# Moving the shared expert of a mixture-of-experts layer from the third phase to the first, and running the first norm of the second layer ahead, in a two-layer decoder on one core

## The chip, the core and the metric

The kernel runs on 1 of the 8 cores of one Trainium2 chip. The metric is the device time of one execution in microseconds. TensorE (PE) does the matmuls and loads its weights beside them (PEld); VectorE (DVE), ScalarE (ACT) and GpSimd (POOL) work on what it leaves; SyncE (SP) issues nearly all DMAs. Each engine runs its own instruction stream in order, and the streams meet at semaphores.

## What is computed

Sixteen sequences of 256 tokens of 128 features pass through two layers; ctx is 64 tokens of 96 features for each sequence.

```python
x = ln(x + L0_attn(x))            # 16 heads of 8, causal
x = ln(x + L0_xattn(x, ctx))      # 8 heads of 16
x = ln(x + L0_ffn(x))             # router: 6 of 64 experts, at most 64 tokens each, and the shared expert
x = ln(x + L1_attn(x))            # 16 heads of 64, causal
x = ln(x + L1_xattn(x, ctx))      # 16 heads of 64
x = ln(x + L1_ffn(x))             # attention over four nested slices, 8 heads of 16
# in L0_ffn the shared expert, the part that the change moves:
z = silu(xf @ ws1.T) * (xf @ ws3.T) @ ws2.T      # 128 -> 176 -> 128 features
return (y + z).reshape(shape)                    # y: the sum of the six experts of each token
```

## The kernel before, in words

Everything is fp32 but the scores from which only row maxima are taken. The program has three parts, since an expert can only run when all tokens have been routed.

**Phase one** (`phase1_streams`) takes the sequences in pairs, A (s = 0) and B (s = 1), through L0 and L0X and the router R, 8 iterations. It stores the tokens with their router scores in `xg` in DRAM (192 columns a token, one store a sequence, step RN on SP). **The experts** gather token rows from `xg`, run, and scatter into `zd` (six rows a token). **Phase three** (`phase3_streams`) takes the pairs through the rest. For each sequence it loads the token (`x3_in`) and its six rows (`routed`), and then runs the steps "F": XT transposes the tokens on PE; F1 is the two products with ws1 and ws3, a tanh on ACT and two fused DVE operations; F2 is the product with ws2 and the DVE addition; Z on DVE sums the six rows and adds the token; then come the norm (statistics on DVE, the power of -0.5 on POOL, step L on DVE), and layer 1: XT, Q, K, V, S (scores for the maxima), N (their transpose), T (transposed scores and exp), P (values), D and B (row sums), W (output product).

**The order** of all this is written out by hand. Each phase has four streams of steps, two main ones (A and B) and two of the router or of XT-F1-Z (C and D). A string of turns (`TURNS1`, `TURNS3`) says which stream gives the next step. `AHEAD` says how many steps of each stream belong to the next pair: with (5, 19, 3, 3) the loop body runs the last 79 and 65 steps of the main streams for its own pair and the first 5 and 19 for the next one. Every engine walks the same list. Ahead of the loop the list is walked once for the "ahead" steps alone, and behind it once for the others alone.

PSUM has six units, which rings of the names Q, O, D and M share out (`fills` gives the ring of each step). A unit has a semaphore for full and one for free, and counts must go on where a step is left out. So PE does `absent_step` for every step that the walk leaves out (L917 to L922):

```python
for i in range(len(fills(step))):
    pe.wait_ge(*v.may_fill(step, i))
    pe.sem_inc(v.full(step, i), 1)
    pe.sem_inc(v.free(step, i), 1)
```

That is three instructions of PE's sequencer for each fill. Line numbers below are those of the kernel before: the transpose XT is L506, F1 L904, F2 L913, the product Q L522, K L535, the largest score L1143, exp L1016, Z L1279 and L1283, the norm L1056 to L1075 and L1313, W of L1F L858.

Of the kernel before, what the change touches and what calls it, by code (L numbers as in the profile page):

```python
# [5 lines left out]
FP32 = mybir.dt.float32  # L6
# [11 lines left out]
FI = 88  # L18
# [88 lines left out]
def phase3_streams():  # L107
    shared = lambda s: [("XT", "F", s, 0), ("F1", "F", s, 0), ("Z", "F", s, 0)]
    main = lambda s: ([("F2", "F", s, 0), ("L", "F", s, 0), ("XT", L1, s, 0)] + project_steps(L1, s) + head_steps(L1, s)
# [3 lines left out]
    return [main(s) for s in AB] + [shared(s) for s in AB]  # L113


TURNS1 = ("A B A B A C A4 B A2 B A2 C B2 A D A B C A D B A2 D B C B4 D A B C A B D B D A2 B A B A2 D B A B A "
          "B2 A B D A B A2 B4 A B2 A D A B2 A B2 A2 B2 A")
TURNS3 = ("B A B2 A2 B2 A5 B A B A3 B2 A3 B A B3 A4 B3 A B8 A B3 A3 B A B A B A B A B3 A2 B2 A B A2 B A4 B A3 "
          "B2 A2 B A3 B A B A2 B A B A B A B A4 B2 A2 B A2 B A B2 A B2 A D A B A B A D B C A2 B A B A B A B A "
          "D B3 A2 C A3 B2 A C A B5 A B2 A B4 A B3 A2 B2")  # L120
AHEAD1, AHEAD3 = (36, 31, 0, 0), (5, 19, 3, 3)
# [25 lines left out]
def fills(step):  # L147
# [17 lines left out]
    if kind in ("D", "L", "C", "CK", "RN", "RL", "Z") or kind == "W" and step[3]:  # L165
        return []
# [22 lines left out]
def decoder_program(nc, inp, out):  # L189
    ctx = ExitStack()  # L190
    with ctx:
# [12 lines left out]
        zd = nc.dram_tensor("zd", [TOK * TOPK, D], FP32, kind="Internal").ap()  # L204

# [26 lines left out]
        wx_o2 = sb("wx_o2", [128, 2, 128])  # L232
        wx_o = wx_o2[:, 0, :]
# [4 lines left out]
        ws2 = wx_o2[0:FI, :, :]  # L238
# [8 lines left out]
        w1x_o = sb("w1x_o", [128, 8, 128])  # L247
        b1x_o = sb("b1x_o", [128, 128])
# [57 lines left out]
        rstd = pair("rstd", [128, 4])  # L306
        eps = sb("eps", [128, 4])
# [3 lines left out]
        hid_e = [t[0:FI, 1, 0:512].rearrange("p (c t) -> p c t", c=2) for t in v_big]  # L311

# [27 lines left out]
        class Sync:  # L340


            def __init__(self, tag):
# [16 lines left out]
                if tag == "p1":  # L360
# [4 lines left out]
                    self.key_moved = n("key_moved")  # L365
                    self.sorted = sem(f"{tag}_sorted")
                else:
# [3 lines left out]
                    self.z_link = n("z_link")  # L371
                    self.once_added = n("once_added")
                    self.scaled = n("scaled")
                    self.h_act = n("h_act")
                    self.z_sum = n("z_sum")
# [6 lines left out]
               ("p3", "F"): 0, ("p3", L1): 1, ("p3", L1X): 2, ("p3", L1F): 3}  # L382
        LN_PER = {"p1": 2, "p3": 4}
# [85 lines left out]
        def previous_x(a):  # L469

            return {L0X: L0, "R": L0X, L1: "F", L1X: L1, L1F: L1X}[a]

        def x_source(tag, a, s):

            if a == "F":
                return x3_in[s][:, :, :]
# [13 lines left out]
        def tensor_step(pe, v, step):  # L490
            kind, a, s = step[0], step[1], step[2]
            y, mm = v.y, nc.tensor.matmul
            if kind == "XT":
                if a == "F":
                    pe.wait_ge(y.x_in[s], v.at(16, 16))
                    if not v.first():

                        pe.wait_ge(y.x_ready[s], v.ln(L1X) - LN_PER["p3"])
# [399 lines left out]
            elif kind == "F1":  # L898
                if not v.follows(step, ("XT", "F", s, 0)):
                    pe.wait_ge(*v.drained(("XT", "F", s, 0)))  # L900
                for i in range(2):
                    pe.wait_ge(*v.may_fill(step, i))
                    for c in range(2):
                        last = mm(v.bank(step, i)[0:FI, c * 256:(c + 1) * 256], ws13[:, 2 * i + c, :], xt[s][:, :],  # L904
                                  start=True, stop=True)
                    last.then_inc(v.full(step, i), 1)
            elif kind == "F2":
                if not v.follows(step, ("F1", "F", s, 0), 0, 1):
                    pe.wait_ge(*v.drained(("F1", "F", s, 0), 1))
# [14 lines left out]
        def scalar_step(act, v, step):  # L924
# [27 lines left out]
            elif kind == "K":  # L952
                i, bank = step[3], v.bank(step)
                act.wait_ge(*v.filled(step))
                if a is L1:
                    for j in range(2):
# [122 lines left out]
        def vector_step(dve, v, step):  # L1079
# [111 lines left out]
            elif kind == "L":  # L1191
                if a is L0X:
# [675 lines left out]
```

## Time and profile before

| | |
|---|---|
| time before, median of 3 runs | 2123.05 us (2116.55 to 2128.08) |
| the profiled execution | 2126.89 us, its span 2124.9 us |
| busy, share of the span | PE 82%, PEld 52%, DVE 53%, ACT 42%, POOL 11% |
| mean granted TensorE clock | 0.912 of full speed |
| phase one | about 22 to 558 us |
| the experts | about 558 to 670 us |
| phase three | about 670 us to the end; outputs of a pair 174.0 to 177.5 us apart |

Times are microseconds from the start of the span. A busy PE need not be PE at its peak, since ends of matmuls are modelled. "Idle before" names what ended an engine's idle time; "issue" is time in which it waited for nothing that the profile shows, and PEq is PE's own sequencer.

### The profile page before, as it was taken

Reading aid. Unit: us, or ns where it says so; the run is one execution under the profiler, and the core shown is the slowest. Engines: PE = TensorE matmul, PEld = TensorE weight load, DVE = VectorE, ACT = ScalarE, POOL = GpSimd, SP = SyncE. Lnnn points to the kernel's source line nnn. Section 1 sums busy time; section 2 is a strip of 40 time slices with the busy share of each in tenths; the row PEclk is TensorE's granted clock in tenths of the full one; section 3 lists DMA queues with packets and bytes.
Section 4 is the critical chain, followed back from the end, with each engine's and each line's share of the span. In section 5 each row is a group of like instructions: output and inputs, shape, how many; then the busy total and the mean of one; then the engine's idle time right before and its main releaser. Section 6 shows DMA issues by size and latency. Waiting matters only on the chain.

```text
span 2124.9 us, 49983 instructions
## 1 busy us (share of the span) xinstructions
PE 1741.2 (82%) x20036; PEld 1104.7 (52%) x20052; DVE 1126.7 (53%) x2330; ACT 894.5 (42%) x1625; POOL 228.2 (11%) x392
## 2 busy tenths in 40 slices
PE   3787777777263699899799889989979978988995
PEld 2444444444153366456556556655745655664663
DVE  5567766777532434643662563464356257256434
ACT  2444444454110245444444444544444445445453
POOL 0100011010074000100100100010010010001000
PEclk9879988999575799999999899989989999998998
DMA  8200000000373100100000010010000001000000
GB/s 295 105 16 19 18 18 7 19 14 7 96 92 93 35 2 3 41 2 3 21 22 2 2 41 2 2 40 2 4 21 22 2 2 41 2 2 6 1 2 6
DMA packets 43295, 60.23 MB, mean 28 GB/s; under 512 B 6183, under 2 KB 33297, under 8 KB 42659
## 3 DMA queue, kind: packets, MB, share of 16 engines
q1 hardware_dynamic: 40003, 53.95, 7.9%
q0 software_dynamic: 2560, 3.46, 1.8%
q8 instruction: 141, 2.31, 0.5%
q10 hardware_dynamic: 576, 0.39, 0.1%
q14 instruction: 15, 0.12, 0.0%
HBM read 39.63 MB, written 19.92 MB: 28 GB/s over the span
## 4 chain that ended last, share of the span: by engine, by line
PE 68%; ACT 10%; DVE 9%; issue 8%; DMA 2%; POOL 2%; PEldq 1%; ACTq 0%; DVEq 0%; SPq 0%; POOLq 0%
PE psum L522 7%; PE psum L749 6%; PE psum L864 6%; PE psum L661 5%; ACT prob L1016 5%; PE psum L714 4%; DVE peak L1143 3%; PE psum L547 3%; PE psum L535 3%; PE psum L762 3%; PE psum L817 3%; PE psum L904 2%; PE psum L579 2%; PE psum L656 2%; PE psum L614 2%
## 5 line engine op out<-in xcount | busy, mean ns | idle before, releaser
L1016 ACT ACTIVATE prob<-psum 128x1024 f32<-128x1024 f32 (+2 forms) x384 | 339.9, 915 | 385.8 <-PE psum L668 176.8
L1143 DVE TENSOR_REDUCE peak<-psum 128x4 bf16<-128x1024 f32 (+2 forms) x304 | 366.0, 1223 | 165.7 <-PE psum L590 97.3
L1310 POOL TENSOR_TENSOR rstd<-moments,eps 128x2 f32<-128x2 f32 x96 | 18.7, 195 | 1554.1 <-DVE moments L1061 1554.1
L661 PE MATMUL psum<-qt,kt 64*128 64x256 f32 x1024 | 131.8, 377 | 0.0
L1126 DVE TENSOR_REDUCE peak<-psum 128x8 bf16<-128x512 f32 x64 | 41.3, 688 | 158.5 <-PE psum L597 158.5
L749 PE MATMUL psum<-prob,v_big 128*64 128x256 f32 x1024 | 124.6, 385 | 0.0
L614 PE MATMUL psum<-kb,qb 32*128 32x512 bf16 x320 | 64.3, 416 | 62.1 <-DVE peak L1143 35.8
L1150 DVE RECIPROCAL rsum<-psum 128x128 f32<-128x128 f32 x32 | 30.7, 958 | 152.9 <-PE psum L762 111.7
L714 PE MATMUL psum<-qt,kt 32*128 32x256 f32 (+1 forms) x1536 | 103.4, 392 | 0.0
L817 PE MATMUL psum<-prob,va 128*32 128x256 f32 (+1 forms) x1536 | 97.0, 374 | 5.1 <-ACT prob L1016 4.9
L1172 DVE TENSOR_TENSOR qt<-qt,psum 128x1024 f32<-128x1024 f32 x64 | 78.0, 1219 | 34.5 <-PE psum L844 34.5
L661 PEld LDWEIGHTS psum<-qt,kt 64*128 64x128 f32 x1024 | 87.4, 188 | 8.0
L714 PEld LDWEIGHTS psum<-qt,kt 32*128 32x128 f32 x1536 | 87.5, 218 | 7.0
L973 ACT CAST qb<-qt 128x1024 bf16<-128x1024 f32 (+1 forms) x112 | 86.6, 773 | 1.3
L749 PEld LDWEIGHTS psum<-prob,v_big 128*64 128x64 f32 x1024 | 67.8, 136 | 36.6 <-issue 4.2
L958 ACT ACTIVATE kt<-psum,b_qk 128x256 f32<-128x256 f32 x128 | 53.6, 470 | 78.6 <-PE psum L535 78.2
L1187 DVE TENSOR_TENSOR summed<-psum,x_res 128x256 f32<-128x256 f32 x80 | 33.9, 423 | 80.3 <-PE psum L864 49.2
L535 PE MATMUL psum<-xt,w_qkv 128*128 128x256 f32 x256 | 74.6, 421 | 0.5
L1313 POOL TENSOR_TENSOR rstd<-rstd,power 128x2 f32<-128x2 f32 (+1 forms) x96 | 72.6, 757 | 7.5
L710 PE MATMUL psum<-shift_n,sel_h 32*128 32x384 bf16 (+1 forms) x384 | 39.2, 396 | 40.8 <-ACT prob L1016 20.2
L547 PE MATMUL psum<-w_qkv,xt 128*128 128x512 f32 x128 | 72.3, 648 | 0.0
L864 PE MATMUL psum<-w1x_o,qt 128*128 128x128 f32 x512 | 64.8, 280 | 8.2 <-DVE qt L1172 8.2
(246 smaller groups left out, 3311.1 us busy)
## 6 DMA issues: line engine op xcount, KB each, us to landing
zd<-kx SPq DMA_DIRECT2D x24, 512.0 KB, 6.0
union<-zd SPq DMA_DIRECT2D x16, 768.0 KB, 4.6
xg<-union SPq DMA_DIRECT2D x16, 192.0 KB, 2.0
v_big<-in_w1T SPq DMA_DIRECT2D x4, 704.0 KB, 8.8
prob<-in_w3T SPq DMA_DIRECT2D x4, 704.0 KB, 11.5
kt<-in_w2T SPq DMA_DIRECT2D x4, 704.0 KB
union<-in_x SPq DMA_DIRECT2D x16, 128.0 KB, 2.2
union<-in_xT SPq DMA_DIRECT2D x16, 128.0 KB, 2.2
```

Of the source, the lines that this page charges most:

```text
L522: last = mm(bank[:, j * 256:(j + 1) * 256], w[:, c * 128:(c + 1) * 128], x, start=True, stop=True)
L535: last = mm(bank[:, j * 256:(j + 1) * 256], w1_qkv[:, c * 128:(c + 1) * 128], xt[s][:, :], start=True, stop=True)
L547: last = mm(bank[:, :], xt[s][:, t * 128:(t + 1) * 128], w1_qkv[:, 2048 + 512 * half:2560 + 512 * half], start=True, stop=True)
L614: last = mm(banks[:, jj, :].rearrange("p (i k) -> p i k", i=heads.stop - heads.start), qb[s][r, 0, q0:q0 + 128], kb[s][r, heads, keys], st ...
L661: mm(banks[:, u, j * 256:(j + 1) * 256], kt[s][r, c, ktile * 128:(ktile + 1) * 128], qt[s][r, c, :], start=False, stop=False, skip_group_c ...
L714: last = mm(bank[:, 256 * k:256 * k + 256 - q0], km[a][s][r, g, 128 * k:128 * k + 128], qt[s][r, 0, q0:256], start=False, stop=a is L1F, s ...
L749: last = mm(bank[64 * u:64 * u + 64, j * 256:(j + 1) * 256], v_big[s][:, k, h * 64:(h + 1) * 64], prob[s][:, slot + 2 * k + u, j * 256:(j ...
L817: last = mm(bank[32 * j:32 * j + 32, c + q0:c + 256], lhs, p, start=(g == 0 and k == 0), stop=(k == 1), skip_group_check=True)
L864: last = mm(bank[:, t * 128:(t + 1) * 128], qt[s][:, u, t * 128:(t + 1) * 128], w[:, u, :], start=(u == 0 and t == 0), stop=(u == 7), skip ...
L973: copy(flat(qb[s][:, c, :]), flat(qt[s][:, c, :])).then_inc(y.q16[s], 1)
L1016: nc.scalar.activation(prob[s][:, slot + 2 * i:slot + 2 * i + 2, 0:n], v.pair(step, i)[:, :, 0:n], ACT.Exp, scale=a.scale).then_inc(v.free ...
L1143: nc.vector.tensor_reduce(dst, src, axis=AX.X, op=ALU.max).then_inc(v.free(step), 1)
```

## The change

The shared expert (F1, F2) becomes part of the router's stream in phase one, where it uses the transposed tokens that the router has made. Its output, with the token added, is stored in a new DRAM array `xz` (F2 on SP), and phase three loads `xz` in place of the token columns of `xg`. In phase three a new stream "front" holds Z (the sum of six rows), Y (the addition and the statistics, with semaphores and tiles of their own), L (the norm, in place in `x_ffn`) and the transpose of layer 1's input. All four run ahead for the next pair; the transpose of the tokens for F1 is gone. Turns and AHEAD are new. `w1x_o` holds L0X's output weight in phase one, so L1_Wo is loaded behind the routers, and ws13 and ws2 at the start.

```diff
-    router = lambda s: ([("XT", "R", s, 0)] + [(k, "R", s, 0) for k in ("R1", "RN", "R2", "R3")]
+    router = lambda s: ([("XT", "R", s, 0)] + [(k, "R", s, 0) for k in ("R1", "F1", "RN", "F2", "R2", "R3")]
-    shared = lambda s: [("XT", "F", s, 0), ("F1", "F", s, 0), ("Z", "F", s, 0)]
-    main = lambda s: ([("F2", "F", s, 0), ("L", "F", s, 0), ("XT", L1, s, 0)] + project_steps(L1, s) + head_steps(L1, s)
+    front = lambda s: [("Z", "F", s, 0), ("Y", "F", s, 0), ("L", "F", s, 0), ("XT", L1, s, 0)]
+    main = lambda s: (project_steps(L1, s) + head_steps(L1, s)
-AHEAD1, AHEAD3 = (36, 31, 0, 0), (5, 19, 3, 3)
+AHEAD1, AHEAD3 = (29, 36, 0, 0), (43, 46, 4, 4)
...
+                dve.wait_ge(y.xz_kept[s], v.at(16, 1))
+                tt(xz_out[s], v.bank(step)[:, 0:256].rearrange("p (t d) -> p t d", t=2), xs[s][:, :, 0:D],
+                   ALU.add).then_inc(v.free(step), 1)
+            elif kind == "Z":
                 if not v.first():
-                    dve.wait_ge(y.x_ready[s], v.ln(L1F) - LN_PER["p3"])
...
+                    dve.wait_ge(y.x_ready[s], v.ln(L1X) - LN_PER["p3"])
+                dve.wait_ge(y.routed_in[s], v.at(16, 16))
+                nc.vector.tensor_reduce(x_ffn[s], routed[s].rearrange("p t k d -> p t d k"), axis=AX.X,
+                                        op=ALU.add).then_inc(y.f_link[s], 1)
+            elif kind == "Y":
+                dve.wait_ge(y.f_link[s], v.at(3, 1))
+                dve.wait_ge(y.x_in[s], v.at(16, 16))
+                tt(x_ffn[s], x_ffn[s], x3_in[s][:, :, :], ALU.add).then_inc(y.f_link[s], 1)
...
+            elif kind == "F2":
+                sp.wait_ge(*v.drained(step))
+                sp.dma_start(xz[bass.ds(seq * T, T), :].rearrange("(t p) w -> p t w", p=128), xz_out[s]).then_inc(
+                    y.xz_kept[s], 16)
...
             for q in AB:
                 sp.wait_ge(p1.r_keyed[q], ITERS)
+                sp.wait_ge(p1.xz_kept[q], ITERS * 16 + 1)
```

Three places of PE's order, before and after. Names end in the sequence's number (1 is B, 0 is A), and ident, psum and the weights are common. The first place is the start of phase three, behind the last expert; before:

```order
L506 MATMUL psum<-ident,x3_in1 128x128 x2
L904 MATMUL psum<-xt1,ws13 88x256 x4
L506 MATMUL psum<-ident,x3_in0 128x128 x2
L913 MATMUL psum<-wx_o2,v_big1 128x128 x4
L904 MATMUL psum<-xt0,ws13 88x256 x4
L506 MATMUL psum<-ident,x_tok1 128x128 x2
L522 MATMUL psum<-xt1,w1_qkv 128x256 x4
```

and after, where the new lines L510, L526 and L539 are the old L506, L522 and L535:

```order
L510 MATMUL psum<-ident,kt1 128x128 x2
L526 MATMUL psum<-xt1,w1_qkv 128x256 x4
L539 MATMUL psum<-xt1,w1_qkv 128x256 x4
L510 MATMUL psum<-ident,kt0 128x128 x2
L526 MATMUL psum<-xt1,w1_qkv 128x256 x2
```

The five rows of F ahead of layer 1's first transpose are gone, and that transpose reads the normed tokens in `kt1` at once. The second place is the loop of phase three, in the last module L1F of both sequences; before:

```order
L858 MATMUL psum<-wf_o,kt1 64x128 x4
L913 MATMUL psum<-wx_o2,v_big1 128x128 x4
L690 REGISTER_ALU
L710 MATMUL psum<-shift_n0,sel_h 128x512 x4
L714 MATMUL psum<-qt0,kt0 128x256 x8
L817 MATMUL psum<-prob0,va0 32x256 x8
L904 MATMUL psum<-xt0,ws13 88x256 x2
L902 REGISTER_ALU
L904 MATMUL psum<-xt0,ws13 88x256 x2
L736 REGISTER_ALU
L817 MATMUL psum<-prob0,va0 32x256 x8
```

and after, where L862, L714, L718 and L821 are the old L858, L710, L714 and L817:

```order
L862 MATMUL psum<-wf_o,kt1 64x128 x4
L526 MATMUL psum<-xt1,w1_qkv 128x256 x4
L653 REGISTER_ALU
L714 MATMUL psum<-shift_n0,sel_h 128x512 x4
L718 MATMUL psum<-qt0,kt0 128x256 x8
L821 MATMUL psum<-prob0,va0 32x256 x8
L533 REGISTER_ALU
L539 MATMUL psum<-xt1,w1_qkv 128x256 x4
L507 REGISTER_ALU
L510 MATMUL psum<-ident,kt0 128x128 x2
L740 REGISTER_ALU
L821 MATMUL psum<-prob0,va0 32x256 x8
```

Where F1 and F2 stood between the products of A's L1F, the next B's Q and K of layer 1 stand now. The third place is the loop of phase one; after, with L908 the F1 and L917 the F2 of phase one:

```order
L908 MATMUL psum<-x_out0,ws13 88x256 x2
L906 REGISTER_ALU
L908 MATMUL psum<-x_out0,ws13 88x256 x2
L653 REGISTER_ALU
L714 MATMUL psum<-shift_n1,sel_h 128x384 x4
L718 MATMUL psum<-qt1,kt1 128x256 x4
L718 MATMUL psum<-qt1,kt1 128x128 x4
L728 MATMUL psum<-tri_t,ident_inf 32x2x128 x16
L917 MATMUL psum<-ws2,v_big1 128x128 x4
```

Here F1 of A is followed, one T step later, by F2 of B. Before, no row of ws13 stood in this loop.

## Rows read from the trace of the kernel before

**Rows 1.** Windows: us, busy us (instructions) of PE, PEld, DVE, ACT, POOL, clock, DMA.

```profile
95.40:485.00 389.60, 305.90 (x4426) 180.21 (x4436) 274.72 (x682) 179.00 (x397) 38.68 (x72) 0.89 0.05 16
...
886.00:1940.50 1054.50, 957.00 (x10297) 609.04 (x10296) 531.21 (x936) 482.38 (x805) 85.58 (x168) 0.95 0.05 14
...
1940.50:2124.90 184.40, 157.22 (x1726) 99.80 (x1724) 86.52 (x161) 80.99 (x134) 15.16 (x30) 0.94 0.02 4
```

**Rows 2.** Waits of PE, 886 to 1940.5 us: total, times, longest.

```profile
PE psum L522 <- ACT xt_nested L933: 14.3, 12, 1.4
```

**Rows 3.** Timeline of PE around L1F: start, us, instruction, idle before it.

```profile
1212.37 2.08 PE L522 MATMUL psum<-xt_nested,w_qkv 128*128 128x256 f32 x4 [0.93 <-ACT xt_nested L933]
...
1219.70 3.71 PE L904 MATMUL psum<-xt,ws 128*88 128x256 f32 x8
...
1236.62 2.02 PE L904 MATMUL psum<-xt,ws 128*88 128x256 f32 x8
...
1247.51 1.13 PE L913 MATMUL psum<-wx_o,v_big 88*128 88x128 f32 x8 [0.15 <-ACT kt L958]
```

**Rows 4.** Groups by line: count, busy us, mean ns, idle before.

```profile
L904 PE MATMUL psum<-xt,ws 128*88 128x256 f32 x128 | 46.3, 525 | 1.8 <-PEq L922 1.8
...
L913 PE MATMUL psum<-wx_o,v_big 88*128 88x128 f32 x128 | 19.2, 296 | 5.1 <-PEq L922 3.8 <-ACT kt L958 1.2
```

**Rows 5.** Timeline at the start of phase three.

```profile
669.29 0.48 DVE L1783 MEMSET va<- 128x512 f32 x1
...
678.06 0.90 SPq L1344 DMA_DIRECT2D union<-zd  x2
...
702.56 0.66 PE L506 MATMUL psum<-ident,x_in 128*128 128x128 f32 x2 [37.41 <-PEq L922]
...
705.04 3.44 PE L904 MATMUL psum<-xt,ws 128*88 128x256 f32 x8 [1.81 <-PEq L922]
...
708.51 0.41 PE L506 MATMUL psum<-ident,x_in 128*128 128x128 f32 x2
...
709.19 2.73 DVE L1279 TENSOR_REDUCE kt<-union 128x256 f32<-128x1536 f32 x1
711.95 0.43 DVE L1283 TENSOR_TENSOR kt<-kt,x_in 128x256 f32<-128x256 f32 x1
...
712.76 2.05 PE L913 MATMUL psum<-wx_o,v_big 88*128 88x128 f32 x8 [3.84 <-PEq L922]
...
714.60 3.62 PE L904 MATMUL psum<-xt,ws 128*88 128x256 f32 x8
...
719.58 0.44 PE L506 MATMUL psum<-ident,x_tok 128*128 128x128 f32 x2 [1.36 <-DVE x_tok L1075]
```

**Rows 6.** Timeline of DVE's part of F.

```profile
714.85 0.42 DVE L1289 TENSOR_TENSOR summed<-psum,kt 128x256 f32<-128x256 f32 x1 [2.47 <-PE psum L913]
...
717.18 0.68 DVE L1272 SCALAR_TENSOR_TENSOR v_big<-v_big,psum 88x512 f32<-88x512 f32 x1 [0.99 <-ACT v_big L1049]
```

**Rows 7.** Timeline of the end.

```profile
2116.23 0.66 PE L858 MATMUL psum<-wf_o,kt 128*64 128x128 f32 x8 [0.46 <-ACT kt L1037]
...
2117.39 0.49 DVE L1056 BATCH_NORM_STATS2 stats<-summed 128x6 f32<-128x128 f32 x2
...
2119.44 0.60 DVE L1075 TENSOR_SCALAR x_out<-summed,moments,rstd 128x128 f32<-128x128 f32 x2 [1.16 <-POOL rstd L1313]
```

**Rows 8.** DMA issues: count, KB each, median us from issue to landing.

```profile
union<-zd SPq DMA_DIRECT2D x16, 768.0 KB, 4.6
xg<-union SPq DMA_DIRECT2D x16, 192.0 KB, 2.0
```

**Rows 9.** Timeline of the first waits for weights and for DVE.

```profile
15.52 1.50 POOL L1328 TENSOR_TENSOR x_res<-union,b_o 128x256 f32<-128x256 f32 x2 [14.59 <-DMA x_in<-in_token_key]
...
21.95 2.08 PE L522 MATMUL psum<-union,w_qkv 128*128 128x256 f32 x4 [21.95 <-DVE sel_h L1768]
```

**Rows 10.** The chain that ended last, between routers and experts: start, us.

```profile
569.53 8.92 DMA summed<-kx
```

More of the change, by code:

```diff
@@ L164, in fills @@
         return ["Q"]
-    if kind in ("D", "L", "C", "CK", "RN", "RL", "Z") or kind == "W" and step[3]:
+    if kind in ("D", "L", "C", "CK", "RN", "RL", "Z", "Y") or kind == "W" and step[3]:
         return []
@@ L469, in previous_x @@
         def previous_x(a):
-            return {L0X: L0, "R": L0X, L1: "F", L1X: L1, L1F: L1X}[a]
+            return {L0X: L0, "R": L0X, L1X: L1, L1F: L1X}[a]
         def x_source(tag, a, s):
-            if a == "F":
-                return x3_in[s][:, :, :]
+            if a is L1:
+                return x_ffn[s]
             if a == "R":
@@ L493, in tensor_step @@
             if kind == "XT":
[L494 to L498, printed above, removed]
+                if a is L1:
+                    pe.wait_ge(y.f_x_ready[s], v.once())
                 elif a is L1F:
@@ L903, in tensor_step @@
                     for c in range(2):
-                        last = mm(v.bank(step, i)[0:FI, c * 256:(c + 1) * 256], ws13[:, 2 * i + c, :], xt[s][:, :],
+                        last = mm(v.bank(step, i)[0:FI, c * 256:(c + 1) * 256], ws13[:, 2 * i + c, :], r_xt[s],
                                   start=True, stop=True)
@@ L1191, in vector_step @@
             elif kind == "L":
-                if a is L0X:
+                if a == "F":
+                    dve.wait_ge(y.f_rstd_ready[s], v.at(2, 2))
+                    for t in range(2):
+                        last = nc.vector.tensor_scalar(x_ffn[s][:, t, :], x_ffn[s][:, t, :], moments_f[s][:, t, 0:1],
+                                                       rstd_f[s][:, t:t + 1], ALU.subtract, ALU.mult)
+                    last.then_inc(y.f_x_ready[s], 1)
+                elif a is L0X:
                     dve.wait_ge(y.out_done[s], v.at(16, 1))
+                    dve.wait_ge(y.xz_kept[s], v.at(16, 1))
                     layer_norm_apply(dve, v, s, a, summed[s], xs[s][:, :, 0:D])
@@ L1291, in vector_step @@
-                dve.wait_ge(*v.drained(step))
-                layer_norm_sums(dve, v, s, "F", summed[s])
+                    dve.wait_ge(y.x_ready[s], v.ln(L1X) - LN_PER["p3"])
[6 more added lines that the diff above has]
+                tt(x_ffn[s], x_ffn[s], x3_in[s][:, :, :], ALU.add).then_inc(y.f_link[s], 1)
+                dve.wait_ge(y.f_link[s], v.at(3, 2))
+                for t in range(2):
+                    last = nc.vector.bn_stats(stats_f[s][:, t, :], x_ffn[s][:, t, :])
+                last.then_inc(y.f_link[s], 1)
+                dve.wait_ge(y.f_link[s], v.at(3, 3))
+                carry_wait(dve)
+                for t in range(2):
+                    last = nc.vector.bn_aggr(moments_f[s][:, t, :], stats_f[s][:, t, :])
+                last.then_inc(y.f_moments_ready[s], 1)
@@ L1299, in pool_step @@
             y = v.y
-            if kind == "F2" or kind == "W" and (step[3] or not a.big):
-                which = "F" if kind == "F2" else a
+            if kind == "Y":
+                pool.wait_ge(y.f_moments_ready[s], v.once())
+                nc.gpsimd.tensor_tensor(rstd_f[s][:, :], moments_f[s][:, :, 1], eps[:, 0:2], ALU.add).then_inc(
+                    y.f_rstd_ready[s], 1)
+                pool.wait_ge(y.f_rstd_ready[s], v.at(2, 1))
+                nc.gpsimd.tensor_tensor(rstd_f[s][:, :], rstd_f[s][:, :], power[:, 0:2], ALU.pow).then_inc(
+                    y.f_rstd_ready[s], 1)
+            if kind == "W" and (step[3] or not a.big):
+                which = a
                 pool.wait_ge(y.moments_ready[s], v.ln(which))
```

84 lines of the change are left out of this document (41 added, 43 removed).

## The prediction

> **What bounds the kernel now.** I read the span in windows first, one for the loop of each phase. Six iterations of phase three take 1054.5 us, 175.75 each, and PE is busy for 957.0 of them (91%); DVE is busy for 531 and ACT for 482 [rows 1]. So phase three is bound by PE, and work taken off PE there is worth nearly its own time. Six iterations of phase one take 389.6 us, 64.9 each: PE 305.9 (79%), DVE 274.7 (71%), ACT 179.0 [rows 1]. No engine is full there; PE and DVE hand the lead to each other, and per iteration PE has (389.6 - 305.9) / 6 = 14.0 us of idle time and DVE 19.1. What work added there costs depends on where it falls. The second view is the waits of PE in phase three's loop. The largest is for the nested input of L1F, 14.3 us in 12 waits [rows 2], and the timeline shows the same place in one iteration: PE comes to it late and at the lower clock level. The four matmuls of Q there take 2.08 us, and F1, which comes 7 us later as PE's filler, takes 3.71 us, while the other F1 of the same pair takes 2.02 [rows 3]: half the clock, 1.2 for 2.4 GHz. The third view is the timeline of the two ends. PE is free for phase three when DVE's last memset ends at 669.77, but its first matmul stands at 702.56, and the idle time is its own sequencer's [rows 5].
>
> **Head of phase three.** That idle time is absent_step. In the order before, 106 fills of left-out steps come ahead of the first ahead step: (702.56 - 669.77) / 106 = 0.31 us a fill. After, counted from the new turns in the same way, 54 fills stand there, 16.7 us, so that PE arrives at 686.5. The data are then what is late. The rows of the experts are asked for at 678.06 to 678.96 [rows 5] and land in 4.6 us [rows 8], B's at about 683.1. Z takes 2.7 us, the addition 0.4 [rows 5], links 0.35 in all, and statistics to the end of the norm 2119.44 + 0.60 - 2117.39 = 2.65 us, as at the end of the run [rows 7]. That gives 689.3. The first transpose of layer 1 starts at about 689.7 for 719.58 [rows 5]: **-29.9**. If the landing is 3 us later, 3 us less.
>
> **Work taken off PE in phase three.** Per sequence one transpose, F1 and F2. Over the whole phase F1 is busy for 46.3 us and F2 for 19.2 [rows 4]; sixteen transposes at 0.41 to 0.66 [rows 5] are about 8. Together 73.5 us. Of them 0.66 + 3.44 + 0.41 + 2.05 + 3.62 = 10.2 us stand ahead of 719.58 [rows 5] and are in the first term, so at most 63.3 remain. F1 has its mean of 2.9 us by the low clock of one of two; at full clock a sequence costs 2.02 + 1.13 + 0.44 = 3.59 [rows 3, 5], sixteen of them 57.4, less 6.0 for the same pieces, 51.4. Which it is depends on whether the low stretch goes on to lie on other matmuls. I take the middle: **-57**, 7.1 us an iteration. The transpose of layer 1's input, Z, the additions and the norm stay, on their engines; DVE loses 0.68 + 0.68 + 0.42 a sequence [rows 6], which no one waits for. The norm had no slack before: PE waited 1.36 us for it at 719.58 [rows 5]. It now runs at least ten PE rows ahead of its Q.
>
> **The gaps of L1F.** F was filler there. In the new order the first half of L1F (from Q of B to T of B) has none in its place, and the second half has the next B's Q and K, which are more work than F was. I set the change of the gaps at 0, with -5 to +4 us an iteration as the bounds: the whole wait for the nested input is 14.3 / 6 = 2.4 us an iteration [rows 2], the idle time of an iteration 16.2 [rows 1], and I do not expect a third of it to go or a quarter more to come.
>
> **Tail of phase three.** The new AHEAD is paid at the other end. The walk behind the loop leaves out 89 main and 8 front steps, and 69 fills of them come behind the last W of A; before, it was 18. At 0.31 us a fill 69 are 21.3 us on PE's sequencer, and the program ends when PE does. Before, the end came at 2124.9, 8.0 us behind the last row of L858 (2116.23 + 0.66) [rows 7], through the norm and the last store; 18 fills are 5.6 and hid behind those. So **+13.3**, up to +16 at the 0.35 us a fill that the wait for F2 shows (3.84 us, 11 fills) [rows 5].
>
> **Phase one.** Added per iteration: on PE 2 x (2.02 + 1.13) = 6.3 us at full clock, 2 x (3.62 + 2.05) = 11.3 at half [rows 3, 5]; on DVE 3.6 [rows 6]; two stores of 128 KB, which land in about 2.0 us as the 192 KB ones do [rows 8]. SP waits in its queue for F2's drain ahead of the store; queued behind it are the other sequence's xg store, then context loads that are needed an iteration later, so this wait costs nothing. L0X's norm waits for the previous store, a whole iteration old. No row shows F in this loop, so I bound it. From below: PE has 14.0 us idle per iteration [rows 1], most of it in pieces shorter than F1, and a denser PE could raise the 0.89 of its clock; -1 us an iteration. From above: all of it exposed at the low clock, and 2 us for the ring M, because F2 of B waits for the unit that F1 of A has just filled and DVE empties only behind RN: 13 us. The loop keeps an engine 79% busy, so I take half of the 6.3 exposed and 1.3 for the ring: 4.5 us, times eight, **+36**. At the end of phase one the pieces of F stand in the last chain of A, and L1_Wo adds 424 KB to the loads ahead of the half list, whose move took 8.92 us on the chain [rows 10] against 2.0 for a larger store [rows 8]: together **+5** (0 to 10). At the start ws13 and ws2 join the weights that PE waits for. The last of these now landed by 15.52, and DVE held PE until 21.95 [rows 9]: 6.4 us of cover for two issues and 264 KB. Nothing; if that cover were gone they would cost 2 to 3.
>
> **The sum.** -29.9 - 57 + 13.3 + 36 + 5 = -32.6, against the profiled execution's own 2126.9: 2094. That execution stands 3.8 above the median of the runs shown, so I forecast **2090 us**, 1.5% less.
>
> **The clock, weighed.** The loop's granted clock is 0.95, and in the place where F1 was filler it is at the lower level [rows 1, 3]. If the gaps there grow, more of the iteration runs at that level. Should the mean fall to 0.91, an iteration loses 175 x 0.04 = 7 us, 56 in all, and the sum would be 2146. By the Trainium skill ("TensorE: Matmul & The Clock Gate", Part 1, HAM oscillation) idle gaps of PE throttle it back to half rate, and the work behind each gap then runs slowly until activity has released it again; it speaks against taking filler out of a latency-bound stretch. By that rule the trace agrees, in that Q behind a gap takes twice its time. I hold to the sum since the second half of L1F gets new filler.
>
> **The rivals.**
> 1. F was filler, and its removal saves little. Then an iteration gives 3 us, not 7.1, and the time is 2090 + 33 = 2123, no change. For it: F1 at 1219.70 lies in a stretch where PE waits anyway. Against it: the other F1, at 2.02 us, and both F2 lie in full stretches. 0.13.
> 2. The new order closes gaps as well: the second half of L1F, with Q, K and S of the next B beside it, loses 4 us of idle an iteration; seven of them give 28 and 2062. For it: 16.2 us of idle, and a front that no longer stands in the chain. Against: the first half. 0.17.
> 3. Slower: phase one takes F at its full low-clock price with the waits of ring M, 13 us an iteration; +68 on the forecast, 2158. It decides against the change from 9.8 us an iteration on. For it: F2 of B directly behind F1 of A. Against: 14 us of idle and a clock that density raises. 0.07.
> 4. The clock, above: 2146. 0.05.
>
> **How the numbers follow.** The forecast has 0.58, with its own range of 2070 to 2110. 0.5% of the time, 10.6 us, is about what a measurement of this kernel can tell from no change. Faster by more than that: 0.58 + 0.17 and a little of rival 1: 0.76. Same: 0.13. Slower: 0.11. The range for 8 in 10 leaves out the lowest of rival 2 and rivals 3 and 4: 2052 to 2125.
>
> **What would show it.** First transpose of layer 1 at 688 to 694 (shifted by what phase one gained); some 55 fills of sequencer time ahead of it. PE's last matmul 20 to 25 us ahead of the span's end. Period of phase three 168 to 170 us, clock at 0.95. Period of phase one 68 to 71, with waits of F2 for DVE. The prediction is wrong if the period of phase three stays above 173 or falls under 164, or if phase one grows by less than 1 or more than 9 us an iteration.

## The result and the profile after

The changed kernel took 2134.35 us (median of 20 runs) beside 2120.2 us for the kernel before on the same chip. The ratio is 1.0063, with an interval of 1.0040 to 1.0086: **slower by 0.6%**, where 1.5% faster was forecast. The profiled execution has a span of 2128.3 us against 2124.9, and a clock of 0.895.

Windows of the changed kernel (us, busy us and instructions of each engine, clock, DMA share, GB/s): five periods of phase one from x load to x load, the rest of phase one, six iterations of phase three.

```profile
105.42:466.63 361.21, 290.00 (x3822) 171.70 (x3831) 243.06 (x596) 157.73 (x340) 32.26 (x60) 0.87 0.07 20
466.63:628.09 161.46, 129.19 (x1554) 77.63 (x1556) 106.92 (x283) 65.05 (x145) 13.10 (x25) 0.81 0.06 18
930.34:1936.80 1006.46, 920.10 (x10084) 587.42 (x10080) 511.99 (x900) 469.50 (x781) 89.07 (x169) 0.95 0.05 14
```

Phase three has fallen from 175.75 us an iteration [rows 1] to 1006.46 / 6 = 167.7, at the same clock. Phase one has grown to 361.21 / 5 = 72.2. The kernel before has 64.9 by the same marks, the window here:

```profile
95.42:420.06 324.64, 256.88 (x3662) 151.57 (x3670) 226.05 (x566) 148.88 (x330) 32.24 (x60) 0.87 0.05 16
```

At the start of phase three, the timeline of the changed kernel answers to [rows 5]. At its end, it answers to [rows 7]:

```profile
740.38 0.48 DVE L1812 MEMSET va<- 128x512 f32 x1
749.15 0.90 SPq L1371 DMA_DIRECT2D union<-zd  x2
755.28 2.74 DVE L1299 TENSOR_REDUCE kt<-union 128x256 f32<-128x1536 f32 x1 [14.41 <-DMA union<-zd]
760.58 0.60 DVE L1201 TENSOR_SCALAR kt<-kt,moments_f,rstd_f 128x128 f32<-128x128 f32 x2 [1.18 <-POOL rstd_f L1323]
761.24 0.69 PE L510 MATMUL psum<-ident,kt 128*128 128x128 f32 x2 [24.99 <-DVE kt L1201]
...
2106.11 0.74 PE L862 MATMUL psum<-wf_o,kt 128*64 128x128 f32 x8 [0.46 <-ACT kt L1043]
```

PE now waits for DVE's norm (L1201), no longer for its own sequencer, and starts layer 1 at 761.24, 20.4 us behind the last memset; before it was 49.8. At the end its last matmul stands at 2106.85 and the span ends at 2128.3, 21.4 us later.

With these marks the 3.4 us by which the spans differ are made up completely:

| stretch | before | after | difference |
|---|---|---|---|
| start to the expert loads | 558.78 | 628.09 | +69.3 |
| to the request of the experts' rows (678.06, 749.15) | 119.3 | 121.1 | +1.8 |
| to the first transpose of layer 1 (719.58, 761.24) | 41.5 | 12.1 | -29.4 |
| to PE's last matmul (2116.89, 2106.85) | 1397.3 | 1345.6 | -51.7 |
| to the end | 8.0 | 21.4 | +13.4 |

Four of five stretches lie within 5.3 us of the forecast. The error is in the first: +69.3, where +36 and a part of the +5 were given. Two things stand out in it. The first is the timeline of PE at the place where the loop of phase one begins anew (behind W of L0X for B, L875):

```profile
305.63 0.71 PE L875 MATMUL psum<-w1x_o,kt 128*128 128x128 f32 x4 [0.46 <-ACT kt L1043]
309.94 0.40 PE L644 MATMUL psum<-neg_ident,peak 128*32 128x128 bf16 x8 [3.60 <-issue]
311.00 0.44 PE L699 MATMUL psum<-shift_n,sel_h 32*64 32x256 bf16 x8 [0.66 <-ACT shift_n L1010]
311.19 1.09 PE L703 MATMUL psum<-qt,kt 32*64 32x256 f32 x5
312.64 1.15 PE L703 MATMUL psum<-qt,kt 32*64 32x256 f32 x11 [0.36 <-issue]
313.71 2.08 PE L526 MATMUL psum<-union,w_qkv 128*128 128x256 f32 x4
315.72 1.98 PE L808 MATMUL psum<-prob,vx 128*64 128x256 f32 x8
```

"<-issue" is idle time in which PE waited for nothing that the profile shows: 3.6 us, and 0.36 inside a step that is one row elsewhere. Q behind it takes 2.08 us, nearly twice what it takes at the higher clock level. At the first entry into the loop the same steps follow one another with none of this (L875 at 96.40, L644 at 97.04, Q at 98.67 in 1.13 us): W to Q takes 2.3 us there and 8.1 here. The second is the queue of code in the list of DMA queues (packets, MB, share of 16 engines). It is first the kernel before, then the changed one:

```profile
q8 instruction: 141, 2.31, 0.5%
```

```profile
q8 instruction: 195, 3.19, 0.6%
```

### The profile page after: what moved, and what is told of

Read it like the earlier page. It is cut to its first block, busy times and chain, and to the rows that moved or that the text cites. A ratio compares the mean times of both kernels' runs of the same rounds, so it can differ in the third digit from the quotient of the medians.

```text
span 2128.3 us, 49852 instructions
## 1 busy us (share of the span) xinstructions
PE 1762.4 (83%) x20004; PEld 1116.8 (52%) x20020; DVE 1128.5 (53%) x2330; ACT 891.2 (42%) x1609; POOL 234.7 (11%) x392
## 4 chain that ended last, share of the span: by engine, by line
PE 59%; issue 16%; DVE 14%; ACT 5%; POOL 3%; DMA 2%; SPq 1%; DVEq 0%; ACTq 0%; PEldq 0%; POOLq 0%; PEld 0%
PE psum L753 6%; PE psum L526 5%; DVE peak L1149 5%; PE psum L665 5%; PE psum L868 4%; PE psum L718 3%; PE psum L766 3%; PE psum L551 3%; PE psum L539 3%; PE psum L660 2%; ACT prob L1022 2%; PE psum L583 2%; PE psum L821 2%; PE psum L543 1%; PE psum L618 1%
## 5 line engine op out<-in xcount | busy, mean ns | idle before, releaser
L718 PE MATMUL psum<-qt,kt 32*128 32x256 f32 (+1 forms) x1536 | 107.0, 402 | 0.0
L618 PE MATMUL psum<-kb,qb 32*128 32x512 bf16 x320 | 72.5, 450 | 40.6 <-ACT prob L1022 16.2
L821 PE MATMUL psum<-prob,va 128*32 128x256 f32 (+1 forms) x1536 | 93.6, 363 | 1.8 <-ACT prob L1022 1.6
L718 PEld LDWEIGHTS psum<-qt,kt 32*128 32x128 f32 x1536 | 88.9, 222 | 7.8
L1193 DVE TENSOR_TENSOR summed<-psum,x_res 128x256 f32<-128x256 f32 x80 | 33.8, 423 | 99.3 <-PE psum L868 71.6
L954 ACT COPY qt<-psum 128x512 f32<-128x512 f32 x80 | 46.2, 585 | 81.0 <-PE psum L526 80.0
L526 PE MATMUL psum<-xt,w1x_q 128*128 128x256 f32 x256 | 66.6, 406 | 14.2 <-issue 10.5
L1029 ACT COPY qt<-psum 128x512 f32<-128x512 f32 x64 | 37.5, 585 | 91.3 <-PE psum L753 91.1
L526 PE MATMUL psum<-xt,w_qkv 128*128 128x256 f32 x256 | 70.2, 408 | 2.8 <-PEq L926 2.1
L539 PE MATMUL psum<-xt,w_qkv 128*128 128x256 f32 x256 | 69.8, 401 | 1.1 <-PEq L926 0.6
```

The source lines that it names most:

```text
L526: last = mm(bank[:, j * 256:(j + 1) * 256], w[:, c * 128:(c + 1) * 128], x, start=True, stop=True)
L539: last = mm(bank[:, j * 256:(j + 1) * 256], w1_qkv[:, c * 128:(c + 1) * 128], xt[s][:, :], start=True, stop=True)
L618: last = mm(banks[:, jj, :].rearrange("p (i k) -> p i k", i=heads.stop - heads.start), qb[s][r, 0, q0:q0 + 128], kb[s][r, heads, keys], st ...
L718: last = mm(bank[:, 256 * k:256 * k + 256 - q0], km[a][s][r, g, 128 * k:128 * k + 128], qt[s][r, 0, q0:256], start=False, stop=a is L1F, s ...
L821: last = mm(bank[32 * j:32 * j + 32, c + q0:c + 256], lhs, p, start=(g == 0 and k == 0), stop=(k == 1), skip_group_check=True)
```

## The experiments

Chips differ in the stage of the experts: from its loads to the request of its rows it took 119 to 124 us on some and 144 to 152 on others, for kernels of either order. So stages are compared by their own marks, and whole times by the ratio to the kernel before on the same chip. "Period" is always the mean of five, from x load to x load, as in the windows above; the expectations name some periods up to 1 us shorter (71.6 and 63.9 for 72.2 and 64.9). Theory 1 at first was that PE's branch back costs several us when nothing is queued behind which it hides; its rival (theory 2) was that F's own work is all of the growth.

**1. The loop cut elsewhere.**

```diff
-TURNS1 = ("A2 B A B A D B3 ... A2 B A2 B2 D B")
-AHEAD1 = (29, 36, 0, 0)
+TURNS1 = ("B A B A D B3 ... A2 B A2 B2 D B A2")
+AHEAD1 = (31, 36, 0, 0)
```

> The changed kernel with the loop of phase one cut at another place: the steps N and T of L0X for sequence A, first in the loop's body, stand at its end instead (AHEAD1 31 for 29), so that PE branches back with 16 + 48 instructions of work queued and not with one W. The order of the work is the same. Theory 1 (the back branch of PE's loop costs 4 to 6 us where nothing is queued behind which it hides): the loop's period in phase one falls from 71.6 to 66-68 us, phase one by 28-42 us, the kernel from 2134 to about 2095-2105. Theory 2 (F's own work is all of the growth): period 71.6 +/- 0.5, the kernel within 5 us of the changed one.

The period was 338.86 / 5 = 67.8 us and the expert loads began at 597.89, 30.2 us earlier. Ratio 0.9896 (0.9854 to 0.9938). The same work in the same order was 1.7% shorter, which theory 2 does not allow.

**2. The cut of the kernel before, moved to behind W.**

```diff
-TURNS1 = ("A B A B ... B A2 B2 A")
-AHEAD1 = (36, 31, 0, 0)
+TURNS1 = ("B2 A A B A B ... B A2")
+AHEAD1 = (35, 29, 0, 0)
```

> The kernel before with the cut of phase one's loop moved the other way: N and T of L0X for B and the last L of A stand at the start of the body instead of at its end (AHEAD1 35, 29), so that the loop ends behind L0X's W, with nothing queued. Same work in the same order. Theory 1: the period in phase one grows from 63.9 to 68-70 us, the kernel by 28-42 us (ratio 1.013 to 1.02). Theory 2: 63.9 +/- 0.5 us, ratio 1.000 +/- 0.003.

Period 318.72 / 5 = 63.7 us, the expert loads at 558.34. Ratio 1.0036 (1.0006 to 1.0065), of which phase one shows nothing. With nothing queued at the branch PE ran on without a stall, so theory 1 falls in this form: the empty queue is not what costs.

**3. The order of before with F put in.**

```diff
+def with_f(plan):
+    out = []
+    for step, ahead in plan:
+        kind, a, s = step[0], step[1], step[2]
+        if kind == "R2":
+            out.append((("F2", "R", s, 0), 0))
+        out.append((step, ahead))
+        if a is L0 and (kind, s) in (("T", 0), ("P", 0)) and step[3] == 1:
+            out.append((("F1", "R", 0 if kind == "T" else 1, 0), 0))
+    return out
```

> The changed kernel with phase one in the order of the kernel before (its turns and its cut of the loop), F1 and F2 put in where they stand in no gap by intent: F1 for A behind T of L0's second round, for B behind the second P, F2 ahead of R2. Theory 1: with the cut behind queued work the period is 66-68 us and the kernel 2090-2105. Theory 2: F costs 7.7 us an iteration wherever it stands: period 71-72, the kernel 2125-2140. Theory 3 (the new order of phase one itself is slower, not F and not the cut): period 65-67 here, and the cut alone (the kernel with the loop cut elsewhere) gives nothing.

Period 363.00 / 5 = 72.6 us, expert loads at 631.70, ratio 1.0093 (1.0062 to 1.0124); 141 packets of code. F put into this order costs 72.6 - 64.9 = 7.7 us an iteration, nearly the 8.0 us by which phase three's iteration fell. It is what theory 2 said, but theory 2 had failed in experiment 1.

**4. The changed kernel without F.**

```diff
-        plan = {"p1": interleaved(phase1_streams(), TURNS1, AHEAD1),
+        plan = {"p1": [x for x in interleaved(phase1_streams(), TURNS1, AHEAD1)
+                       if x[0][0] not in ("F1", "F2")],
```

> The changed kernel without F1 and F2 in phase one on any engine, and without their store: the shared expert is left out of the result, phase three loads the tokens where it loaded their sum with the shared expert. Order and cut of the loop are the changed kernel's. Theory 1 (cut 4-6, F 2-4 us an iteration): the period falls to 68-70 us. Theory 2 (F is all of it): to 63.9-64.5. Theory 3 (the order): stays over 70.

Period 355.94 / 5 = 71.2 us, expert loads at 617.89, 136 packets, ratio 1.0011 (0.9979 to 1.0043). Only theory 3 gave such a period, and it had failed in experiments 1 and 3, where the cut alone gave 30 us and the old order nothing. Some 160 matmuls in five periods are gone, and the period is longer than that of experiment 1 with F.

**What the four have in common.** Of the kernels so far only the changed one has 195 packets; the others have 136 to 141, and none of theirs lie between 175 and 530 us. The queue of code of the changed kernel in that stretch:

```profile
q8 instruction: 44, 0.72, 0.8%
```

That is 9 packets of 16 KB in each iteration. PE's loop has 1,633 instructions of 64 bytes, 102 KB or 6.4 pieces of 16 KB; it is the only loop in the phase that is longer than a piece. The Trainium skill ("Runtime: NRT & Kernel Launch", Instruction fetch mechanics) says that PE holds 128 KB of code, refilled in blocks of 16 KB; a note there has only two blocks held and a fetch at every branch out of them. The traces here speak against the note: PE's loops of 98 and 102 KB jump back without a packet in every kernel so far but the changed one. By the figure of 128 KB a loop that touches seven blocks leaves one to fetch into, and one that touches eight leaves none. That was theory 4, and position alone tests it.

**5. Nothing but PE's code moved.**

```diff
+            for _ in range(80):
+                pe.sem_inc(pad, 1)
             pe.wait_ge(consts_ready, 1)
```

> The changed kernel with 80 increments of an unused semaphore ahead of PE's first wait, which ends at about 57 us and hides them. Nothing else differs; PE's code behind them lies 5,120 bytes further on. Theory 4 (code): the changed kernel's loop of phase one is fetched anew in every iteration (195 instruction packets of 16 KB in all, some 10 an iteration, against 141 and none between 170 and 580 us in the kernel before and in every kernel run so far), because of where its 1,633 instructions of 64 bytes begin in the 16 KB pieces of code; moved on, they stay. Then 141 packets or so, no stall of 3.6 us behind W of L0X, a period near 68.3 us as where the loop was cut elsewhere, the expert loads at 598-602 us instead of 628.1, the kernel 25-32 us shorter than the changed one (ratio about 0.99). Theory 1 (an empty queue at the back branch): no change, period 71.6, expert loads at 628, ratio 1.004 to 1.009.

Expert loads at 594.35, 33.7 us earlier; ratio 0.9875 (0.9831 to 0.9919). The page has

```profile
q8 instruction: 135, 2.21, 0.4%
```

and the window of the five periods, and PE where the loop begins anew, are

```profile
105.46:441.60 336.14, 280.41 (x3820) 170.47 (x3828) 242.53 (x595) 157.94 (x340) 32.33 (x60) 0.90 0.06 19
```

```profile
296.69 0.71 PE L875 MATMUL psum<-w1x_o,kt 128*128 128x128 f32 x4 [0.46 <-ACT kt L1043]
297.33 0.30 PE L644 MATMUL psum<-neg_ident,peak 128*32 128x128 bf16 x8
298.29 0.32 PE L699 MATMUL psum<-shift_n,sel_h 32*64 32x256 bf16 x8 [0.66 <-ACT shift_n L1010]
298.39 0.64 PE L703 MATMUL psum<-qt,kt 32*64 32x256 f32 x16
298.96 1.13 PE L526 MATMUL psum<-union,w_qkv 128*128 128x256 f32 x4
```

The stall is gone and Q behind it is at full clock; W to Q is 2.3 us, as in straight code. The period is 67.2 us for 72.2. The first x load of the loop is at 105.46 for 105.42, so the increments themselves cost nothing.

**6. The same edit, moved by a whole piece of 16 KB.** The number is 256 instead of 80.

> The changed kernel with 256 increments ahead of PE's first wait: 16,384 bytes, one whole piece of code, where 80 of them (5,120 bytes) ended the fetching in phase one's loop. Theory 4 (what counts is where the loop lies within its 16 KB pieces): the place within a piece is that of the changed kernel again, so the loop is fetched anew in every iteration: 190 to 200 packets, a period of 71 to 72 us, a stall of 3 to 5 us at the loop's start, expert loads at 625-630 us, ratio 1.003 to 1.01. Theory 5 (any shift of the start ends it, by other timing): about 140 packets, expert loads at 594-600, ratio 0.985 to 0.99.

196 packets, period 362.15 / 5 = 72.4 us (x loads at 120.22 and 482.37), 3.08 us "<-issue" at the same L644. The increments cost 14.8 us here (120.22 - 105.42), so the expert loads at 641.56 are 626.8 without them. Ratio 1.0152 (1.0094 to 1.0211), of which 14.8 us or 0.7% are the increments. Theory 4 holds and theory 5 falls: one piece further on, the fetches, the stall and the period are as in the changed kernel. The stall in one iteration:

```profile
253.08 0.41 PE L644 MATMUL psum<-neg_ident,peak 128*32 128x128 bf16 x8 [3.08 <-issue]
```

**7 and 8. The other cut, moved on by 154 and by 205.**

> The changed kernel with its loop cut behind N and T of L0X (which ran at a period of 68.3 us), and 154 increments ahead, PE's code 9,856 bytes further on. Theory 4: the code now lies across one piece of 16 KB more and is fetched anew in every iteration: about 195 packets, the period back at 71 us or more or, if 16 + 48 queued instructions hide the fetch, at 68.3 with the packets there all the same; expert loads at 598 to 628 us. Theory 1: 141 packets, 68.3 us, 598 us.

> The kernel with the loop cut behind N and T of L0X and 205 increments ahead. With none of them no iteration was fetched anew, with 154 two of seven. A refinement of theory 4: what decides is how many instructions of the loop reach into an eighth piece of 16 KB; by the bounds that the runs so far leave, 154 put 5 to 33 there, 205 put 56 to 84 there, and the changed kernel has 46 to 74. So here all or nearly all iterations are fetched anew, 185 or more packets, the period 71 us or more. If the refinement is wrong: 140 to 160 packets and expert loads below 605.

With 154: 159 packets, period 68.4, expert loads at 600.65, ratio 0.9945 (0.9914 to 0.9977). Theory 4 had said all iterations and some 195 packets; the extra packets come in two of the seven only, at about 160 to 220 us and 430 to 500 us. One kernel so shows both cases, behind the 64 queued matmuls of T, where the cut now is. First PE at a start with fetch, then at one without:

```profile
429.31 0.61 PE L703 MATMUL psum<-qt,kt 32*64 32x256 f32 x16
434.90 2.07 PE L526 MATMUL psum<-union,w_qkv 128*128 128x256 f32 x4 [4.98 <-issue]
436.90 1.98 PE L808 MATMUL psum<-prob,vx 128*64 128x256 f32 x8
```

```profile
362.84 1.08 PE L703 MATMUL psum<-qt,kt 32*64 32x256 f32 x16
363.84 2.01 PE L526 MATMUL psum<-union,w_qkv 128*128 128x256 f32 x4
365.78 1.08 PE L808 MATMUL psum<-prob,vx 128*64 128x256 f32 x8
```

The queued work did not shorten the stall, which is 4.98 us here. Q is slow behind the other start too (2.01 us), so its low clock there is not the fetch's doing; but one step later L808 is at full clock without the fetch (1.08 us) and not with it (1.98). With 205: 196 packets, all iterations, period (475.76 - 112.28) / 5 = 72.7, expert loads at 636.30, of which 9.5 are the increments.

**9. The kernel before, moved on by 225.**

> The kernel before with 225 increments ahead of PE's first wait (about 57 us), its code 14,400 bytes further on; nothing else differs. Theory 4: its loop of phase one, 1,568 instructions, now lies across one piece of 16 KB more and is fetched in every iteration: about 195 packets instead of 141, a period of 66 to 68 us instead of 64, expert loads at 573-590 us instead of 558.8, ratio 1.007 to 1.015. Theory 1: 141 packets, 558 us, ratio 1.000 +/- 0.003.

142 packets, period 310.21 / 5 = 62.0 us, expert loads at 558.07. Ratio 1.0115 (1.0050 to 1.0179): the increments delay the first x load by 13.6 us (108.98 for 95.42), and this accounts for two thirds of the 21 us that the medians differ by; what the rest is stays open. The expectations have PE's first wait end at about 57 us, which is wrong: its first matmul stands at 21.95 in the kernel before and at 35.59 here, so most of the increments are in the open. Nothing is fetched anew, against what theory 4 said; between 1 and 28 instructions of the loop reach into an eighth piece here, the fewest of all that reach into one.

The period also shows how much the same order varies with nothing fetched: 64.9 us at a granted clock of 0.87 before, 63.7 at 0.90 with the cut moved, 62.0 at 0.96 here. A difference of 2 or 3 us between two periods can be this. The step with the fetches is larger and goes with them in every kernel of the new order with F: 72.2, 72.4 and 72.7 us with all fetched, 67.2, 67.4 and 67.8 with none.

All kernels in which PE loops, with the place of its loop in the compiled program (first instruction, number of instructions; both are counted in the compiled file):

| kernel | first, length | in an eighth piece | packets | fetched anew | period |
|---|---|---|---|---|---|
| before | 1481, 1568 | - | 141 | none | 64.9 |
| its cut moved | 1420, 1569 | - | 141 | none | 63.7 |
| before + 225 | 1706, 1568 | 1-28 | 142 | none | 62.0 |
| changed | 1432, 1633 | 48-75 | 195 | all | 72.2 |
| changed + 80 | 1512, 1633 | - | 135 | none | 67.2 |
| changed + 80, shorter end | 1512, 1633 | - | 135 | none | 67.4 |
| changed + 256 | 1688, 1633 | 48-75 | 196 | all | 72.4 |
| cut moved | 1493, 1633 | - | 141 | none | 67.8 |
| cut moved + 154 | 1647, 1633 | 7-34 | 159 | 2 of 7 | 68.4 |
| cut moved + 205 | 1698, 1633 | 58-85 | 196 | all | 72.7 |
| order of before, F | 1493, 1637 | - | 141 | none | 72.6 |
| changed without F | 1419, 1565 | - | 136 | none | 71.2 |
| changed without F + 80 | 1499, 1565 | - | 141 | none | 71.2 |

The third column is worked out, not measured. Some code d stands ahead of what the program counts. Two rows bound d: the kernel before stays in seven pieces of 256 instructions only from d = 55 on (1481 + 55 = 6 x 256), its moved cut up to d = 82 (1420 + 1569 + 82 below 12 x 256). This takes it that "none fetched" means seven pieces, which the row of before + 225 puts in doubt. If a few instructions in an eighth piece are let pass, any d from 43 to 93 keeps every loop that is never fetched below every one that always is, and the loops that are always fetched have 36 or more there. The rule that fits every row is then that a loop with many instructions in an eighth piece, from some 36 to 50 on, is always fetched anew, and one with fewer sometimes or never. Where between, and why "sometimes", is open.

**10. The absent steps behind the end left out.**

```diff
                 for n, (step, ahead) in enumerate(plan[tag]):
                     if ahead in aheads:
                         do_step(eng, View(tag, it, ahead), step)
+                    elif last and n > end:
+                        continue
                     elif do_step is tensor_step:
```

> The kernel with the 80 increments ahead, and in phase three's last walk PE no longer marks the steps that lie behind its last own one as absent. Term of the tail in the forecast: the end comes 8 us behind PE's last W instead of 21.4, so 13.3 us less than the kernel with the increments alone, and the rest alike. Rival: another end takes its place (the store of the last result, or the other engines' own ends), and less than 5 us are saved.

With the 80 increments too: 2107.94 us against 2119.43 of experiment 5 on the same chip, 11.5 less; ratio 0.9822 (0.9779 to 0.9865). In the profiles the end stands 8.0 us behind PE's last matmul (2096.39 + 1.12, span 2105.5) and 21.2 with the steps (2096.27 + 1.08, span 2118.6). The term of the tail is right and can be had back.

**11. Without F once more, moved on by 80.**

> The changed kernel without F1 and F2 and their store (the shared expert is left out), with 80 increments ahead. Without them the period was 71.7 us at a clock of 0.81, though no code was fetched and F's work was gone, longer than the 67 us of the kernel with F and 80 increments. If that is F's absence itself (gaps where F stood, PE slower for it): 70 to 72 us again, clock 0.80 to 0.84. If it was a chance of how the clock fell into that run: 62 to 66 us, clock 0.88 or more, which would make F's price 2 to 5 us an iteration.

Period 355.81 / 5 = 71.2 us again, the same to 0.03 us on another chip at another place. This is its window, to be read against that of experiment 5:

```profile
104.02:459.83 355.81, 273.74 (x3662) 157.28 (x3671) 225.96 (x566) 152.25 (x330) 32.24 (x60) 0.81 0.05 15
```

PE has 158 matmuls fewer, is busy for 6.7 us less, and the stretch is 19.7 us longer, at a clock of 0.81 for 0.90. The largest wait in experiment 4's loop is DVE's for S of L0 (L627), 49.4 us in 20 waits; in the changed kernel it was 5.5 in 11. In this order F is filler: taking it out leaves gaps and a slow PE. That the clock is the cause and not only goes with it is argued here, not shown.

**12. PE's two loops written out, with the shorter end.**

```diff
-            with eng.Fori(0, ITERS - 1) as it:
-                body(it, (0, 1))
+            if do_step is tensor_step:
+                for it in range(ITERS - 1):
+                    body(it, (0, 1))
+            else:
+                with eng.Fori(0, ITERS - 1) as it:
+                    body(it, (0, 1))
```

> The changed kernel with PE's two loops written out, so that PE takes no branch at all in either phase, and with the absent steps at the very end left out; the other engines loop as before. PE's code grows from 11,588 to about 41,500 instructions, each fetched once. If the cost of the fetch is the jump back and not the fetching (the first entry into the loop, in straight code, showed no stall): phase one as with the code at rest (period 66 to 68.5, expert loads at 592-602), phase three 1.5 to 2 us less an iteration than 167.6, the kernel 8 to 14 us under the one with 80 increments and the shorter end, ratio 0.975 to 0.98. Rival (the fetching itself costs, by its transfers or because it runs late): phase one near 71 us an iteration as the changed kernel's, ratio about 0.995.

2074.43 us (2059.47 to 2090.17) beside 2118.9 for the kernel before on the same chip: ratio **0.9803 (0.9749 to 0.9857)**, faster than both. Its windows for the five periods of phase one and six iterations of phase three, and its queue of code over the whole span:

```profile
102.77:432.30 329.53, 273.79 (x3822) 167.01 (x3831) 242.05 (x596) 157.48 (x340) 32.37 (x60) 0.93 0.07 21
890.58:1879.31 988.73, 912.59 (x10084) 582.65 (x10080) 511.78 (x900) 469.62 (x781) 89.29 (x169) 0.96 0.05 14
```

```profile
q8 instruction: 162, 2.65, 0.5%
```

Phase one has 65.9 us a period though PE's code is fetched through all of it (33 packets from 175 to 530 us), no longer than where the loop is held (67.2). So what costs is not the fetching but the jump back to code that is not held. Phase three goes from 167.7 to 164.8, more than the 1.5 to 2 us expected. Its loop, 3,517 instructions or 13.7 pieces, never fits; in the changed kernel the waits of PE had this row for its start, and here it is gone:

```profile
PE psum L526 <- issue: 10.5, 6, 2.0
```

That is 1.75 us an iteration of the 2.9. Writing the loops out also takes out every register instruction of PE (49 in an iteration of phase one and 100 in one of phase three, counted in the compiled file), since its waits then have constants. No run separates what this gives from what the missing jump gives.

## Why the prediction was wrong

- **The step that failed is "Phase one", +36.** It took the loop of before, added F's work and the ring's wait, and put two things at nothing: PE's code, and the new order of phase one itself. Measured were +69.3 up to the expert loads. Of that, 33.7 us go when PE's code is moved by 80 instructions and nothing else is changed (experiment 5), and come back with 256 (experiment 6): code fetched anew in each iteration, with a stall at the jump back.
- **What is left, +35.6, lies near the 41 given, but by luck.** It is not F's price. It consists of 10.0 us until the first x load (105.46 for 95.42), 11.5 over five periods (67.2 for 64.9) and 14.0 from there to the expert loads (152.7 for 138.7). The first part has no F in it: no matmul of F starts before 105.46, and PE runs 740 matmuls there in either kernel, at another clock.

```profile
0.00:95.42 95.42, 53.51 (x740) 29.92 (x742) 49.31 (x102) 31.04 (x60) 6.75 (x19) 0.96 0.64 220
0.00:105.42 105.42, 61.45 (x740) 33.76 (x743) 49.20 (x102) 31.34 (x60) 8.98 (x19) 0.87 0.57 195
```

The first line is the kernel before, the second the changed one. Without F at all (experiment 4) the expert loads began at 617.89, 59.1 us behind those of before, and at 618.85 in experiment 11; with F, and nothing fetched (experiment 5), at 594.35, 23.5 earlier. So the new order costs 59.1 us without F, and F in it takes 23.5 off. In the order of before (experiment 3) F costs 72.9 us (631.70 for 558.78), twice the term, again with nothing fetched. The term had neither of the two right, and no run shows why the new order is slow without F; that its clock of 0.81 is the cause is argued in experiment 11.

- **"From above 13 us an iteration, below -1"** held for the loop as a whole (7.3), but not for F alone, and it hid how much the order decides. F costs 7.7 us a period in the order of before (experiment 3) and -4.0 in the new one (67.2 with, 71.2 without, experiments 5 and 11); without F the new turns are 6.3 us a period longer than the old ones. With the spread of experiment 9 in mind, the signs are safe and the sizes are so to 3 us.
- **Head of phase three, -29.9.** Measured -29.4; data late instead of the sequencer, as said: 20.4 us behind the memset, 19.9 forecast.
- **Off PE in phase three, -57, and gaps 0.** Together -51.7. The period is 167.7, 8.0 less, where 7.1 was given, but only in part for the reason given: PE's busy time fell by 6.2 us an iteration, and its idle time, set at no change, by 1.9 (97.5 us to 86.4 in six iterations), a part of what rival 2 said. The walks outside the six iterations kept the rest. Rival 1 and the clock's rival fall: the clock is still 0.95 [rows 1].
- **Tail, +13.3.** Measured +13.4, and 13.2 back when the absent steps are left out.
- **The experts.** +1.8. With it phase one and the experts have +71.1 for the 41 given.
- **The sum.** -32.6 forecast, +3.4 measured between the profiles: 36.0 off, of which 33.7 are code fetched anew. Rival 3, slower by waits of ring M, gave 2158 and another mechanism. The stated bound of 9 us an iteration was not reached: the loop grew by 7.3, the rest of phase one's growth lies at its two ends (+10.0 and +22.7). Rival 3 says that the change turns into a loss from 9.8 us an iteration on; by the forecast's own sum it does so from 4.5 + 32.6 / 8 = 8.6, and 71.1 / 8 is 8.9.

The Trainium skill has the number that would have raised the question (128 KB for PE, and a fetch at a branch), in "Runtime: NRT & Kernel Launch", Instruction fetch mechanics. The loop grew from 98 to 102 KB and came to start 49 instructions earlier, and experiment 5 shows that with another start the 102 KB are held too. The trace of before had both signs: no packet of code between 175 and 530 us, in the loop that was held, and the price at the start of its loop of phase three, whose 3,599 instructions are not held (among the waits of PE from 886 to 1940 us):

```profile
PE psum L579 <- issue: 12.4, 6, 2.3
```

## What to carry to other kernels

A loop whose code is near what its engine holds can have a cliff that is not in any term for the work (5 us of 67 here): look at the queue of instruction packets over the loop, before a change adds instructions or moves code ahead of it. If packets come back in each iteration, move the start, shorten the body, or write the loop out; here straight code was fetched in time. Price an order and its filler together, since the same work cost 7.7 us a period in one order and took 4.0 off in another, and count what an ahead order leaves behind at the very end.

## What was unexpected of the hardware

- 5,120 bytes of increments ahead of a loop of 1,633 PE instructions changed its period from 72.2 to 67.2 us, and 16,384 bytes changed it back to 72.4.
- The stall at the jump back to code that is not held was 3.1 to 5.0 us in phase one, in the places shown, and about 2 us in phase three (12.4 / 6 before, 10.5 / 6 after). The work behind it ran at 1.2 GHz (Q in 2.08 us for 1.13), and 64 queued matmuls did not make it shorter.
- Code of PE in a straight line, some 6 pieces in 65.9 us, had no stall where the loops began, and the period was no longer than with the loop held.
- A loop with less work for PE was slower, and at a lower clock: 71.2 us at 0.81 without F, 67.2 at 0.90 with it.
- The same work in the same order had a granted clock of 0.87 or 0.96, with nothing changed but 225 increments ahead: 64.9 us a period and 62.0, from one profile each.
- 80 increments ahead of the first wait were free, 205 cost 9.5 us, 225 cost 13.6 and 256 cost 14.8.
